# The dispatch logits of the first eight token tiles are made at the head of attention instead of at the start of dispatch

## The chip, the cores and the metric

The kernel runs on one core of a Trainium2 chip. The metric is the device time of one execution in microseconds (us), the median of the runs. The core has a tensor engine (TensorE, PE in the rows), a vector engine (VectorE, DVE), a scalar engine (ScalarE, ACT), GpSimd (POOL) and SyncE (SP), whose queue issues nearly all DMA transfers here. Each engine works through its own instructions in order and waits on semaphores.

## What is computed

A transformer block in fp32 on x of shape (4, 2048, 256): causal grouped-query attention (16 heads of 16, four groups of keys and values), and beside it a soft mixture of 16 experts with 64 slots each. Both read the layer norm of x.

```python
att = jnp.einsum('bsgmd,btgd->bgmst', q, k) / scale      # causal, softmax, times v, times wo
logits = jnp.einsum('bnd,esd->bnes', x, se)              # 2048 tokens x 1024 slots per batch
dispatch = jax.nn.softmax(logits, axis=1)                # over tokens
combine = jax.nn.softmax(logits.reshape(b, n, -1), axis=-1)   # over slots
slots = jnp.einsum('bnd,bnes->besd', x, dispatch)
gate = gelu(slots @ Wg + bg); up = slots @ Wu + bu; eout = (gate * up) @ Wd + bd
out = x + attention + combine @ eout
```

## The kernel before

There are five blocks, and all engines meet between them: `project` (norm, queries, keys, values; it also stores the normed and turned tokens as `y_cols`), `attend`, `dispatch`, `experts`, `combine`.

`attend` handles 16 pairs of batch and key group (`bg`), each in 40 steps, so steps 0 to 639, with a lead of 22 steps (-22 to -1) ahead. `program(s)` lists what TensorE does in step s: four products of keys and queries (`"s"`, L890), whose exponentials ScalarE takes (L809), four products of queries and keys whose row maxima VectorE takes (`"x"`, L903, L857 and L863), and the products with the values of two steps before (`"a"`, L932). The maxima run 22 steps ahead of the products that use them, so the lead holds only maxima: 88 of them. Results go through a ring of seven PSUM banks (`att_ring`), filled in the order of the program; whoever fills a bank waits for the reader of what was in it. When the last maximum of a chunk of 512 queries is made, GpSimd splits the negated maxima in two parts (L778, L780), TensorE turns them three steps later (`"m"`, L909), VectorE copies them (L874), and SyncE writes them as extra rows into the queries (L719). In the lead that happens for chunk 0 in step -16 and for chunk 1 in step -8.

The queries and keys of key groups 1 to 3 have rows that must be zero. ScalarE sets them with twelve copies at the head of `attend` (L799, L801). SyncE loads group 1 in step -6, group 2 in step 6, group 3 in step 46 (`FIRST_LOADS`, `load_group`, L528 to L537): 17 transfers each.

`dispatch` makes, per batch, the logits of 16 tiles of 128 tokens x 1024 slots (phase `"L"`): per tile twelve products on TensorE (L1246: two halves of the slots, two halves of D, three of high and low parts), one copy on ScalarE (L1108), one exponential on ScalarE (L1081, stored as `slot_exps`), and on VectorE one row maximum (L1166) and one running column maximum (L1174). It then multiplies with the tokens (phase `"P"`). The order is L0, L1, P0, L2, P1 and so on. The columns come in chunks of four tiles in three buffers (`yTl`, `yTh`), which GpSimd splits into a high and a low part; the first three chunks are loaded and split at the end of `attend` (L733, L746, L748).

Of the kernel before, what the change touches and what calls it, by code (L numbers as in the profile page):

```python
# [46 lines left out]
HL = GS // NRG  # L47
VW = 32
# [43 lines left out]
def project(nc, w, io, scr, g0):  # L92
# [3 lines left out]
    with ExitStack() as ctx:  # L96
        a = Alloc(nc, ctx, "proj")
        passed = a.sem("passed")
        x = a.sb("x", [P, NX, TPC, D])
        xn = a.sb("xn", [P, 2, TPC, D])  # L100
# [5 lines left out]
        part = a.sb("part", [P, 2, 3, 2, CH], F32R)  # L106
# [413 lines left out]
def load_group(sp, scr, b, g, qs, ks, v, loaded, zeroed):  # L520


    for j in range(len(Q_PART)):
        for rg in range(NRG):
            r = slice(RG * rg + HD * j, RG * rg + HD * (j + 1))
            if b == 0 and zeroed and HD * j >= 32:
                sp.wait_ge(zeroed, 2 * NRG)
# [12 lines left out]
def attend(nc, w, scr, g0, cols):  # L540
# [37 lines left out]
    FIRST_LOADS = {-6: 1, 6: 2, 46: 3}  # L578
    first = [u for u in range(NU) if u == 0 or UNITS[u - 1][0] != UNITS[u][0]]
# [71 lines left out]
    with ExitStack() as ctx:  # L651
        a = Alloc(nc, ctx, "att")
        passed = a.sem("passed")
        qs = [g0["qs"]] + [a.sb(f"qs{g}", [P, CPB, HL * CH], F32R) for g in range(1, NKV)]
# [16 lines left out]
        zeroed = [sem(f"zeroed{g}") for g in range(NKV)]  # L671
# [4 lines left out]
        acc_zeroed, v_ones = sem("acc_zeroed"), sem("v_ones")  # L676
        (sT_ready, exp_done, mask_done, pv_done, mb_ready, mb_used, m_step, nm_ready,
# [4 lines left out]
        def wait_bank(pe, e):  # L682
# [3 lines left out]
            kept = [x[1] * CPB + x[2] + 1 for x in before.get(e, ()) if x[0] == "c"]  # L686
            if exps:
                pe.wait_ge(exp_done, max(exps))
# [9 lines left out]
        with nc.Block() as block:  # L698
            @block.sync
            def _(sp):  # L700
                def load(b, g):
                    for _ in load_group(sp, scr, b, g, qs[g], ks[g], v[g], loaded[g], zeroed[g]):
                        pass
# [5 lines left out]

                for s in ALL_STEPS:  # L710
                    if s in FIRST_LOADS:
                        load_first(FIRST_LOADS[s])
                    for e in program(s):
# [7 lines left out]
                        elif e[0] == "c":  # L721
# [4 lines left out]
                                         cn[:, c]).then_inc(c_out[c], 16)  # L726
                    bg = (s - AV_LAG) // NU
# [3 lines left out]
                    if s == STEPS - NU:  # L731
                        for n in range(RING):
                            sp.dma_start(cols["low"][:, n].bitcast(F32),  # L733
                                         scr["yT_in"][n // CPB, n % CPB]).then_inc(cols["in"][n], 16)
# [4 lines left out]
            def _(pool):  # L739
                def split_columns(k):  # L740

                    n, d = divmod(k, DK)
                    hi, lo = cols["high"][:, n, d], cols["low"][:, n, d]
                    if d == 0:
                        pool.wait_ge(cols["in"][n], 16)
# [4 lines left out]

                for g in range(NKV):
                    nc.gpsimd.memset(v[g][:, :, HD, :], 1.0).then_inc(v_ones, 1)
                for s in ALL_STEPS:
                    if STEPS - 8 * RING * DK // 2 <= s < STEPS and (s - STEPS) % 4 == 0:
# [29 lines left out]
            def _(act):  # L784
# [10 lines left out]
                for g in range(1, NKV):  # L795
                    for rg in range(NRG):
                        r = slice(RG * rg + 32, RG * (rg + 1))
                        zero = w["causal"][r, 0:1]
                        nc.scalar.copy(qs[g][r].rearrange("p c n -> p (c n)"),  # L799
                                       zero.to_broadcast([32, CPB * HL * CH])).then_inc(zeroed[g], 1)  # L800
                        nc.scalar.copy(ks[g][r], zero.to_broadcast([32, S])).then_inc(zeroed[g], 1)  # L801
                for s in ALL_STEPS:
                    if 0 <= s < STEPS:
# [19 lines left out]
            def _(dve):  # L823
# [18 lines left out]
                nc.vector.memset(acc[:], 0.0).then_inc(acc_zeroed, 1)  # L842
                for s in ALL_STEPS:
# [859 lines left out]
```

## Time and profile before

| | us |
|---|---|
| median of three runs | 2695.19 (2692.81 to 2697.54) |
| the profiled execution, its own time | 2698.62 |
| its span in the profile | 2696.9 |
| `project` | 0 to 157 |
| `attend`: lead, then steps 0 to 639 | 159 to 202, 202 to 1760 |
| `dispatch`: L0, L1, then the rest | 1762 to 1809, 1809 to 1873, to about 2215 |
| granted TensorE clock, mean | 0.98 |

The table is in microseconds from the first instruction. A granted clock of 1.0 is 2.4 GHz, 0.5 is 1.2 GHz. Times of instructions are those of one profiled execution.

### The profile page before, as it was taken

The numbers are of one execution on the slowest core, as the hardware profiler recorded it, in microseconds if no ns is written. First come the engines' busy times: TensorE is split into PE (matmuls) and PEld (weight loads), VectorE is DVE, ScalarE is ACT, GpSimd is POOL, SyncE is SP. The second block draws the span as 40 slices with busy tenths as digits, with TensorE's granted clock in tenths as the row PEclk, the third lists the DMA queues.
The fourth block names the chain that finished last, engine by engine and source line by source line (L and its number), as shares of the span: only waits on it lengthen the run. The fifth ranks groups of instructions, "written<-read, shape, count | busy, mean of one in ns | idle before, by whom it ended". The sixth has DMA issues, their size and how long they took to land. (4 is left out here: it accounts for less than half of the span.)

```text
span 2696.9 us, 47797 instructions
## 1 busy us (share of the span) xinstructions
PE 2583.9 (96%) x16291; PEld 1542.2 (57%) x16291; DVE 2048.5 (76%) x4879; ACT 1728.3 (64%) x3510; POOL 427.1 (16%) x676
## 2 busy tenths in 40 slices
PE   7989999999999999999999999998989989999999
PEld 4544444444444444444444444376877878889999
DVE  7779889989998998998898998477465513356665
ACT  4567777777777777777777777966666652222221
POOL 6701111111111111111111111323120100100000
PEclk9969999999999999999999999999999999999999
DMA  7945423303312321330330000044333354545654
GB/s 247 324 111 60 58 29 45 44 12 41 45 24 27 45 34 17 45 44 6 45 44 6 10 6 31 7 181 168 124 134 145 102 168 147 175 152 194 194 193 151
DMA packets 175855, 245.10 MB, mean 91 GB/s; under 512 B 57205, under 2 KB 129017, under 8 KB 174105
## 3 DMA queue, kind: packets, MB, share of 16 engines
q1 hardware_dynamic: 160088, 227.73, 33.8%
q10 hardware_dynamic: 15552, 14.68, 1.8%
q8 instruction: 114, 1.87, 0.3%
q14 instruction: 101, 0.82, 0.1%
HBM read 156.21 MB, written 84.97 MB: 89 GB/s over the span
## 5 line engine op out<-in xcount | busy, mean ns | idle before, releaser
L809 ACT ACTIVATE att_pr<-att_ring 128x512 f32<-128x512 f32 (+3 forms) x2560 | 1174.3, 550 | 333.9 <-PE att_ring L890 326.6
L857 DVE TENSOR_REDUCE att_mx<-att_ring 128x1 f32<-128x512 f32 x1536 | 967.5, 679 | 76.6 <-PE att_ring L903 74.2
L903 PE MATMUL att_ring<-att_ks,att_qs 48*128 48x512 f32 (+3 forms) x1920 | 648.4, 422 | 16.3 <-ACT att_pr L809 7.0
L890 PE MATMUL att_ring<-att_qs,att_ks 64*128 64x512 f32 (+3 forms) x1920 | 578.2, 407 | 5.8 <-DVE att_mx L863 2.3
L890 PEld LDWEIGHTS att_ring<-att_qs,att_ks 64*128 64x128 f32 x1920 | 300.5, 186 | 402.7 <-DVE att_mx L857 148.3
L863 DVE CUSTOM_DVE_ANT_0 att_junk<-att_ring,w_causal 128x256 bf16<-128x256 f32 (+3 forms) x1024 | 466.1, 486 | 59.5 <-PE att_ring L903 34.1
L932 PE MATMUL att_acc<-att_pr,att_v 128*17 128x512 f32 (+3 forms) x3840 | 454.3, 544 | 3.9 <-ACT att_cT L820 1.5
L903 PEld LDWEIGHTS att_ring<-att_ks,att_qs 48*128 48x128 f32 x1920 | 306.9, 185 | 141.6 <-ACT att_pr L809 102.0
L760 POOL TENSOR_SCALAR_AFFINE_SELECT att_pr<-att_pr 128x512 f32<-128x512 f32 x256 | 162.5, 635 | 1035.5 <-ACT att_pr L809 1035.4
L903 PE MATMUL att_ring<-g_ks,g_qs 48*128 48x512 f32 (+3 forms) x640 | 227.1, 465 | 15.6 <-PEq L152 5.7
L1513 ACT CAST com_e1h<-com_tp 128x1024 fp32r<-128x1024 f32 x64 | 64.8, 1017 | 236.2 <-PE com_tp L1573 236.2
L890 PE MATMUL att_ring<-g_qs,g_ks 64*128 64x512 f32 (+3 forms) x640 | 198.4, 410 | 2.5 <-DVE att_mx L863 0.8
L1589 PE MATMUL com_mp<-pre_parts,com_e1h 128*128 x1024 | 186.3, 282 | 4.0 <-DVE com_e1l L1538 4.0
L890 PEld LDWEIGHTS att_ring<-g_qs,g_ks 64*128 64x128 f32 x640 | 103.6, 188 | 135.1 <-DVE att_mx L857 51.3
L1589 PEld LDWEIGHTS com_mp<-pre_parts,com_e1h 128*128 128x128 f32 x1024 | 158.4, 190 | 4.8 <-issue 4.8
L932 PE MATMUL att_acc<-att_pr,g_v 128*17 128x512 f32 (+3 forms) x1280 | 152.0, 547 | 0.0
L903 PEld LDWEIGHTS att_ring<-g_ks,g_qs 48*128 48x128 f32 x640 | 110.7, 201 | 68.5 <-ACT att_pr L809 29.3
L1589 PE MATMUL com_mp<-pre_parts,com_e1l 128*128 x512 | 144.5, 282 | 0.0
L932 PEld LDWEIGHTS att_acc<-att_pr,att_v 128*17 128x17 f32 x3840 | 78.2, 117 | 114.4 <-ACT att_pr L809 72.8
L1246 PE MATMUL dis_ps<-w_seTh,w_yTh 128*128 128x512 f32 x256 | 106.1, 414 | 20.1 <-ACT dis_lg L1108 11.1
L1263 PE MATMUL dis_ps<-dis_y,dis_lg 128*128 128x257 f32 x512 | 114.9, 386 | 7.3 <-ACT dis_lg L1061 7.3
L1263 PE MATMUL dis_ps<-dis_y,pre_parts 128*128 128x257 f32 x512 | 112.6, 380 | 4.5 <-ACT pre_parts L1061 4.5
(170 smaller groups left out, 3272.5 us busy)
## 6 DMA issues: line engine op xcount, KB each, us to landing
slot_exps<-dis_e SPq DMA_DIRECT2D x64, 512.0 KB, 2.7
com_e<-slot_exps SPq DMA_DIRECT2D x64, 512.0 KB, 3.5
att_qs<-q_parts SPq DMA_DIRECT2D x72, 256.0 KB, 12.0
q_parts<-proj_part SPq DMA_DIRECT2D x32, 512.0 KB, 5.1
dis_y<-in_L_attn_x_dram SPq DMA_DIRECT2D x64, 256.0 KB, 2.8
att_ks<-k_parts SPq DMA_DIRECT2D x72, 128.0 KB, 12.6
y_cols<-proj_yT SPq DMA_DIRECT2D x16, 512.0 KB, 5.5
context<-att_cn SPq DMA_DIRECT2D x64, 128.0 KB, 2.0
```

Source lines behind the costliest of these rows:

```text
L760: nc.gpsimd.affine_select(out=blk, in_=blk, compare_op=ALU.is_ge, fill=0.0, base=0, pattern=[[0, GS], [1, P]], channel_multiplier=-1).then ...
L809: nc.scalar.activation(pr[:, s % NPR, h, off:CH], spot(("s", s, h)), ACT.Exp, scale=float(HD) ** -0.5).then_inc(exp_done, 1)
L857: nc.vector.tensor_reduce(dst, spot(e), AX.X, ALU.max).then_inc(mb_used, 1)
L863: nc.vector.tensor_tensor_reduce(junk[:, h % 2, 0:wd], spot(e), w["causal"][:, CH - wd:CH], 1.0, LOW, ALU.add, ALU.max, dst).then_inc(mb_u ...
L890: nc.tensor.matmul(spot(e), ks[g][r, kb * P:(kb + 1) * P], qs[g][r, c, hf * CH + off:(hf + 1) * CH], start=True, stop=True).then_inc(sT_re ...
L903: nc.tensor.matmul(spot(e), qs[g][r, c, q0:q0 + P], ks[g][r, j * CH:j * CH + wd], start=True, stop=True).then_inc(mb_ready, 1)
L932: last = nc.tensor.matmul(acc[VW * h:VW * h + HD + 1, off:CH], v[bg % NKV][:, kb // TPC, :, kb % TPC], pr[:, n % NPR, h, off:CH], start=(n ...
L1246: last = nc.tensor.matmul(ps[:, i % 2, 2 * (t % 2) + h, :], lhs[:, n % RING, k, (t % TPC) * P:(t % TPC + 1) * P], w[rhs][:, k, h * 512:(h ...
L1263: last = nc.tensor.matmul(ps[:, i % 2, q, 0:D + 1], lgs[b % 2][:, t, (hf * HB + q) * P:(hf * HB + q + 1) * P], y[:, m % NY, t % 2, 0:D + 1 ...
L1513: nc.scalar.copy(e1h[:, q].rearrange("p s n -> p (s n)"), tp[:, q, 0:2, :].rearrange("p a n -> p (a n)")).then_inc(e1h_kept, 1)
L1589: last = nc.tensor.matmul(mp[:, q, 0:D], lhs[:, q, s, :], rhs[:, b, s, :], start=(s == 0 and rhs is eoh and lhs is e1h), stop=(s == SB - 1 ...
```

## The change

Eight tiles (`NE`), two chunks of columns, of batch 0 leave phase L0.

- At the head of `attend`, SyncE loads their two chunks of columns, GpSimd splits them, and steps -18 to -3 each get one entry `"l"`: six products that make half a tile of logits (512 slots) in one bank of the ring. ScalarE copies each to the buffer of the exponentials, which is idle in the lead, and SyncE stores each in a new DRAM tensor `first_logits`. ScalarE waits at step 0 until all 16 stores have landed.
- At the end of `attend`, SyncE loads these logits into the queries of key groups 0 and 1, which are done with, and VectorE takes the row and column maxima of the eight tiles in the steps that have no maxima of attention left.
- In `dispatch`, SyncE loads the eight tiles again, to where phase P reads them. L0 makes tiles 8 to 15 only. The exponentials of all 32 tiles of L0 and L1 are spread over the 24 tiles that are left.
- The twelve copies that set rows to zero become twelve GpSimd memsets: two ahead of the column split, the others one per step from step -22 on, ahead of the split of the maxima of that step.
- The queries of the four groups are one tensor, `queries`; a buffer of `project` lies in it, and `nr` and `cm` move to where both blocks reach them.

```diff
+NE = 8
+NEC = NE // TPC
@@ attend
+    NL = 2 * NE
+    L_FROM = -LEAD + 4
@@ program(s)
+        early = [("l", s - L_FROM)] if 0 <= s - L_FROM < NL else []
-        out = [st[0], xs[0], st[1], xs[1]] + ev + [xs[2], st[2], st[3], xs[3]] + av
+        out = [st[0], xs[0], st[1], xs[1]] + ev + [xs[2], st[2], st[3], xs[3]] + early + av
@@ SyncE
+                for n in range(NEC):
+                    sp.dma_start(cols["low"][:, n].bitcast(F32), scr["yT_in"][0, n]).then_inc(cols["in"][n], 16)
                 for s in ALL_STEPS:
                     if s in FIRST_LOADS:
                         load_first(FIRST_LOADS[s])
...
+                        elif e[0] == "l":
+                            k = e[1]
+                            sp.wait_ge(l_kept, k + 1)
+                            sp.dma_start(scr["first_logits"][k // 2, :, k % 2 * 512:(k % 2 + 1) * 512],
+                                         half_tile(k)).then_inc(l_out, 16)
...
+                    if s == STEPS - NU + AV_LAG:
+                        sp.wait_ge(l_out, 16 * NL)
+                        sp.wait_ge(pv_done, (NBG - 4 + -(-NE // 4)) * NU)
+                        for t in range(NE):
+                            sp.dma_start(lg[:, t, :], scr["first_logits"][t]).then_inc(l_in, 16)
@@ GpSimd
+                side = zeros()
+                for _ in range(2):
+                    next(side)
+                for n in range(NEC):
+                    pool.wait_ge(cols["in"][n], 16)
+                    hi, lo = cols["high"][:, n], cols["low"][:, n]
+                    nc.gpsimd.tensor_copy(hi, lo.bitcast(F32)).then_inc(l_split, 1)
+                    pool.wait_ge(l_split, 2 * n + 1)
+                    nc.gpsimd.tensor_tensor(lo, lo.bitcast(F32), hi.bitcast(F32), ALU.subtract).then_inc(l_split, 1)
+                    pool.wait_ge(l_split, 2 * n + 2)
...
                 for s in ALL_STEPS:
+                    if s < 0:
+                        made = sum(len(m_events(u)) for u in range(-LEAD, s))
+                        if made:
+                            pool.wait_ge(nm_ready, made)
+                        next(side, None)
@@ ScalarE
+                    for e in program(s):
+                        if e[0] == "l":
+                            act.wait_ge(mb_ready, turn[e] + 1)
+                            if e[1] >= NPR * GS:
+                                act.wait_ge(l_out, 16 * NPR * GS)
+                            nc.scalar.copy(half_tile(e[1]), spot(e)).then_inc(l_kept, 1)
+                    if s == 0:
+                        act.wait_ge(l_out, 16 * NL)
@@ VectorE: logit_maxes() waits for l_in, then a row maximum and a column maximum per tile, 16 instructions;
@@ one of them per step without maxima, two in odd steps
@@ dispatch
+        first_tile = lambda b: 0 if b else NE
+        SLOTS = 2 * TPB - NE
+        exps_by = lambda b, t: min(-(-2 * TPB * (b * TPB + t + 1 - NE) // SLOTS), b * TPB + t)
+                for t in range(NE):
+                    sp.dma_start(lgs[0][:, t, :], scr["first_logits"][t]).then_inc(l_in[min(t, 1)], 16)
...
+                    if b == 0 and t < 2:
+                        act.wait_ge(l_in[t], 16 if t == 0 else 16 * (NE - 1))
```

How the program's order changes, at three places. First GpSimd from the start of `attend` to the first split of maxima. Before:

```order
L738 UNCONDITIONAL_BRANCH
L752 MEMSET g_v 128x4x4
L752 MEMSET att_v 128x4x4 x3
L778 CAST att_nml<-att_nm 128x2x8
L780 TENSOR_TENSOR att_nml<-att_nm,att_nml 128x2x8
```

And now, in the changed program (`w_queries` and `att_ks` are the zeroed rows):

```order
L791 MEMSET w_queries 32x4096
L789 MEMSET att_ks 32x2048 [waits att_zeroed]
L801 CAST w_yTh<-w_yTl 128x1024 [waits w_yT_in0,att_zeroed]
L803 TENSOR_TENSOR w_yTl<-w_yTl,w_yTh 128x1024 [waits att_l_split]
L801 CAST w_yTh<-w_yTl 128x1024 [waits w_yT_in1,att_l_split]
L803 TENSOR_TENSOR w_yTl<-w_yTl,w_yTh 128x1024 [waits att_l_split]
L806 MEMSET g_v 128x4x4 [waits att_l_split]
L806 MEMSET att_v 128x4x4 [waits att_v_ones] x3
L791 MEMSET w_queries 32x4096 [waits att_v_ones]
L789 MEMSET att_ks 32x2048 [waits att_zeroed]
L791 MEMSET w_queries 32x4096 [waits att_zeroed]
L789 MEMSET att_ks 32x2048 [waits att_zeroed]
L838 CAST att_nml<-att_nm 128x2x8 [waits att_nm_max,att_zeroed]
```

The first split of maxima, which came behind four small memsets, now stands behind six large memsets and two column splits.

Second, TensorE in steps -17 and -16 of the changed program (L982 are products for maxima, L991 to L993 the logits, L999 the turn of chunk 0's maxima; before, the L982 kind and L999's stand alone):

```order
L982 MATMUL att_ring<-g_ks,w_queries 128x512 [waits att_mb_used] x4
L991 MATMUL att_ring<-w_seTh,w_yTh 128x512 [waits att_l_split,att_mb_used]
L992 MATMUL att_ring<-w_seTl,w_yTh 128x512
L993 MATMUL att_ring<-w_seTh,w_yTl 128x512
L991 MATMUL att_ring<-w_seTh,w_yTh 128x512
L992 MATMUL att_ring<-w_seTl,w_yTh 128x512
L993 MATMUL att_ring<-w_seTh,w_yTl 128x512
L982 MATMUL att_ring<-g_ks,w_queries 128x512 [waits att_mb_used]
L982 MATMUL att_ring<-g_ks,w_queries 128x512 [waits att_l_kept]
L999 MATMUL att_ring<-w_ident,att_nml 32x128 [waits att_nm_ready,att_mb_used]
L982 MATMUL att_ring<-g_ks,w_queries 128x384 [waits att_mb_used] x2
```

All that follows in TensorE's order stands behind the wait for the split columns and the wait for the split maxima.

Third, SyncE around step -6 of the changed program (L750 are the stores of logits, L532 to L541 the load of group 1, of which six alternating pairs stand there):

```order
L739 DMA w_queries<-att_mrow 2x8x128 [waits att_mb_used]
L739 DMA w_queries<-att_mrow 2x8x128
L750 DMA first_logits<-att_pr 128x512 [waits att_l_kept] x2
L532 DMA w_queries<-q_parts 16x4x1024
L533 DMA att_ks<-k_parts 16x2048
...
L534 DMA att_v<-v_rows 128x4x64
L541 DMA att_ks<-w_ones 1x32x64 x4
L750 DMA first_logits<-att_pr 128x512 [waits att_l_kept] x4
```

Twelve stores are issued ahead of the load of group 1, the last four behind its 17 transfers.

## Rows read from the trace of the kernel before

**Rows 1.** The page: busy time, share of the span, instructions.

```profile
PE 2583.9 (96%) x16291; PEld 1542.2 (57%) x16291; DVE 2048.5 (76%) x4879; ACT 1728.3 (64%) x3510; POOL 427.1 (16%) x676
```

**Rows 2.** Windows: stretch, length, busy by engine, then clock, DMA share, GB/s.

```profile
200.00:205.00 5.00, 4.98 (x10) 2.28 (x9) 5.00 (x13) 1.19 (x2) 0.00 (x0) 0.50 0.98 109
210.00:220.00 10.00, 9.79 (x65) 4.01 (x63) 9.04 (x23) 7.04 (x17) 2.04 (x5) 0.81 0.41 44
```

**Rows 3.** Timeline of TensorE in the lead: start, us, engine, line, operation.

```profile
158.95 3.50 PE L903 MATMUL att_ring<-g_ks,g_qs 48*128 48x256 f32 x13 [5.73 <-PEq L152]
162.93 3.06 PE L903 MATMUL att_ring<-g_ks,g_qs 48*128 48x384 f32 x8 [0.48 <-DVE att_mx L863]
...
169.01 0.40 PE L909 MATMUL att_ring<-w_ident,att_nml 128*32 128x128 f32 x1
...
202.22 0.76 PE L890 MATMUL att_ring<-g_qs,g_ks 64*128 64x512 f32 x1
```

**Rows 4.** Timeline of VectorE: chunk 1's first maximum, chunk 2's first, first idle time.

```profile
166.53 0.69 DVE L857 TENSOR_REDUCE att_mx<-att_ring 128x1 f32<-128x512 f32 x1
...
183.95 0.68 DVE L857 TENSOR_REDUCE att_mx<-att_ring 128x1 f32<-128x512 f32 x1
...
212.99 0.42 DVE L863 CUSTOM_DVE_ANT_0 att_junk<-att_ring,w_causal 128x256 bf16<-128x256 f32 x1 [0.96 <-PE att_ring L903]
```

**Rows 5.** Timeline of ScalarE at step 0: its first exponentials.

```profile
203.01 0.60 ACT L809 ACTIVATE att_pr<-att_ring 128x512 f32<-128x512 f32 x1 [11.58 <-PE att_ring L890]
...
205.82 1.25 ACT L809 ACTIVATE att_pr<-att_ring 128x512 f32<-128x512 f32 x3 [1.07 <-PE att_ring L890]
```

**Rows 6.** Timeline of GpSimd: its memsets in `project`, a column split in `dispatch`.

```profile
24.41 3.50 POOL L329 MEMSET g_qs<- 32x4096 f32 x1
34.84 1.84 POOL L332 MEMSET g_ks<- 32x2048 f32 x1
...
1790.62 1.04 POOL L1193 CAST w_yTh<-w_yTl 128x1024 fp32r<-128x1024 f32 x1 [6.40 <-DMA w_yTl<-y_cols]
1791.74 2.41 POOL L1195 TENSOR_TENSOR w_yTl<-w_yTl,w_yTh 128x1024 fp32r<-128x1024 f32 x1
```

**Rows 7.** Timeline of SyncE's queue: group 2's first transfer, a store behind it.

```profile
217.79 0.40 SPq L528 DMA_DIRECT2D att_qs<-q_parts  x1
...
227.88 0.58 SPq L725 DMA_DIRECT2D context<-att_cn  x1
```

**Rows 8.** DMA issues with KB and us to landing: 188 to 240 us, whole span.

```profile
context<-att_cn SPq DMA_DIRECT2D x1, 128.0 KB, 13.7
...
context<-att_cn SPq DMA_DIRECT2D x64, 128.0 KB, 2.0
```

**Rows 9.** Timelines of TensorE and ScalarE in L0.

```profile
1762.19 0.76 PE L1246 MATMUL dis_ps<-w_seTh,w_yTh 128*128 128x512 f32 x1 [3.95 <-PEq L698]
...
1767.35 1.01 ACT L1108 COPY pre_parts<-dis_ps 128x1024 f32<-128x1024 f32 x1 [8.69 <-PE dis_ps L1246]
...
1773.86 1.15 ACT L1081 ACTIVATE dis_e<-pre_parts,dis_nr 128x1024 f32<-128x1024 f32 x1
...
1809.35 1.02 ACT L1108 COPY pre_parts<-dis_ps 128x1024 f32<-128x1024 f32 x1 [0.65 <-PE dis_ps L1246]
```

**Rows 10.** Windows: the fastest stretch of loads, in `project`.

```profile
9.00:12.00 3.00, 2.05 (x10) 1.65 (x9) 2.63 (x11) 1.64 (x6) 2.29 (x8) 1.00 1.07 333
```

**Rows 11.** End of attention: timelines of SyncE and VectorE.

```profile
1655.93 1.35 SPq L733 DMA_DIRECT2D w_yTl<-y_cols  x3
...
1719.36 0.28 DVE L874 CAST att_mrow<-att_ring 32x128 fp32r<-32x128 f32 x1 [3.58 <-PE att_ring L909]
1733.71 0.25 DVE L840 RECIPROCAL att_rz<-att_cc 128x16 f32<-128x16 f32 x1 [14.07 <-ACT att_cc L792]
```

**Rows 12.** L1: ScalarE's eight norms in one go, TensorE's wait behind them.

```profile
1833.81 4.04 ACT L1071 ACTIVATE dis_y<-dis_y,w_yb,w_ys 128x256 f32<-128x256 f32 x8
...
1838.80 0.50 PE L1246 MATMUL dis_ps<-w_seTh,w_yTh 128*128 128x512 f32 x1 [1.48 <-ACT dis_lg L1108]
```

More of the change, by code:

```diff
@@ L47 @@
 HL = GS // NRG
+NE = 8
+NEC = NE // TPC
+QW = CPB * HL * CH
 VW = 32
@@ L670, in attend @@
         loaded = [g0["loaded"]] + [sem(f"loaded{g}") for g in range(1, NKV)]
-        zeroed = [sem(f"zeroed{g}") for g in range(NKV)]
+        zeroed = sem("zeroed")
         m_rows = [sem(f"m_rows{c}") for c in range(CPB)]
@@ L686, in wait_bank @@
             kept = [x[1] * CPB + x[2] + 1 for x in before.get(e, ()) if x[0] == "c"]
+            early = [x[1] + 1 for x in before.get(e, ()) if x[0] == "l"]
+            if early:
+                pe.wait_ge(l_kept, max(early))
             if exps:
@@ L904, in _ @@
                                              ks[g][r, j * CH:j * CH + wd], start=True, stop=True).then_inc(mb_ready, 1)
+                        elif e[0] == "l":
+                            t, h = divmod(e[1], 2)
+                            wait_bank(pe, e)
+                            pe.wait_ge(l_split, 2 * (t // TPC) + 2)
+                            at, to = slice(t % TPC * P, (t % TPC + 1) * P), slice(h * 512, (h + 1) * 512)
+                            for k in range(DK):
+                                hi, lo = cols["high"][:, t // TPC, k, at], cols["low"][:, t // TPC, k, at]
+                                nc.tensor.matmul(spot(e), hi, seTh[:, k, to], start=(k == 0), stop=False)
+                                nc.tensor.matmul(spot(e), hi, seTl[:, k, to], start=False, stop=False)
+                                last = nc.tensor.matmul(spot(e), lo, seTh[:, k, to], start=False, stop=(k == DK - 1))
+                            last.then_inc(mb_ready, 1)
                         elif e[0] == "m":
@@ L936, in _, with dispatch @@
                             last.then_inc(pv_done, 1)
-def dispatch(nc, w, io, scr, pre, cols):
+def dispatch(nc, w, io, scr, pre, cols, first_logits):
     HB = SB // 2
@@ L957, in dispatch @@
         e1 = a.sb("e1", [P, 2, NS])
-        nr, zr = a.sb("nr", [P, 2, TPB]), a.sb("zr", [P, 2, TPB])
-        cm = a.sb("cm", [P, 2, NS])
+        nr, cm, nr_ready, cm_done = (first_logits[n] for n in ("nr", "cm", "nr_ready", "cm_done"))
+        zr = a.sb("zr", [P, 2, TPB])
         rz = a.sb("rz", [P, SB])
@@ L1026, in _ @@
                         b = ph[1]
-                        for t in range(TPB):
+                        for t in range(first_tile(b), TPB):
                             if t % TPC == TPC - 2:
@@ L1073, in norm_rows, with token_exps @@
                         normed = m + 1
+                exps = 0
+                def token_exps(stop):
+                    nonlocal exps
+                    for n in range(exps, stop):
+                        token_exp(n // TPB, n % TPB)
+                    exps = max(exps, stop)
                 def token_exp(b, t):
+                    if b == 0 and t < 2:
+                        act.wait_ge(l_in[t], 16 if t == 0 else 16 * (NE - 1))
                     act.wait_ge(nr_ready, b * TPB + t + 1)
@@ L1160, in _ @@
                             slots(i - 1, turned)
-                        for t in range(TPB):
-                            n = b * TPB + t
+                        for t in range(first_tile(b), TPB):
+                            n = b * TPB + t - NE
                             dve.wait_ge(lg_ready, n + 1)
@@ L1206, in _ @@
                         column_maxes(b - 1)
-                    for n in range(b * CPB, b * CPB + CPB):
+                    for n in range(b * CPB if b else NEC, b * CPB + CPB):
                         split(n + RING)
@@ L1607, in block_kernel @@
     s_d = dram("slots", [B - 1, SB, P, D])
+    l_d = dram("first_logits", [NE, P, NS])
     io = {
@@ L1670, in block_kernel @@
                    "parts": parts}
-            dispatch(nc, w, io, scr, pre, cols)
+            dispatch(nc, w, io, scr, pre, cols, first_logits)
             com = combine_inputs(late, nc, io, scr)
```

129 lines of the change are left out of this document (86 added, 43 removed).

## The prediction

> **What bounds the kernel now.** I read the page first: TensorE is busy for 96% of the span [rows 1], so work taken from it should pay, but a share is an average over stages. So I read windows and timelines of the two places the change touches. In the lead the reader is to see that TensorE runs at 1.2 GHz and that VectorE has no gap (5.00 of 5.00 us busy [rows 2]): the maxima set the pace. Chunk 1's eight steps take VectorE from 166.53 to 183.95, 2.18 us a step [rows 4]. VectorE stays gapless until its first idle 0.96 us at 212.99 [rows 4], so everything that holds it up between 159 and 213 lengthens the kernel. After that, TensorE and VectorE are both nearly full [rows 2], and no slack further on takes up a delay. In L0 TensorE is the bound: ScalarE waits for it 0.65 us per tile, and the copies run from 1767.35 to 1809.35 for 15 tiles, 2.80 us a tile [rows 9], so a half tile costs 1.40 us at 2.4 GHz. At 1.2 GHz I take six times 512 columns, 2.6 us.
>
> **Head, part 1: the split columns.** GpSimd starts at 158.9 and does 3.50 + 1.84 (memsets) + 1.04 + 2.41 (split of chunk 0) [rows 6]; with about 0.1 between, the first logits may start at 168.0. The columns themselves land by then (512 KB, issued at once). TensorE gets there after 20 products, at about 165.7 [rows 3]. It waits 2.3 us, and the half tile takes until 170.6. Step -17 follows: four products (1.7) and a half tile (2.6 or less), then two products of step -16: about 175.
>
> **Head, part 2: the split maxima.** In step -16 TensorE must turn chunk 0's maxima. GpSimd goes on from 168.0 with chunk 1's split (3.6), four small memsets (0.8) and the four memsets of steps -22 to -19 (3.50 + 1.84 + 3.50 + 1.84, with gaps 11.0) [rows 6], and only then splits the maxima (0.5): 183.9. Before, TensorE turned them at 169.01 [rows 3]. It now waits some 9 us, with everything behind it, and turns them at 184.0: 15.0 late. VectorE runs dry meanwhile.
>
> **Head, part 3: the rest of the lead.** Before, 33.2 us passed from there to step 0 (169.01 to 202.22 [rows 3]). After: TensorE comes from an idle stretch, so at 1.2 GHz: the rest of step -16 and step -15 are 3.3 + 3.8, less about 1 if the clock rises within it: 6. Then twelve steps with four products and a half tile at 2.4 GHz: 0.8 + 1.4 = 2.2, about VectorE's own 2.18, so 26.6; the two steps without logits 4.4. Sum 37.0: step 0 starts at 221.0 against 202.2, 18.8 late. The second turn (step -8, about 203) is not late: GpSimd's last six memsets end at about 201. ScalarE's zeroing is no gain, since it waited for 11.58 us ahead of the first exponential anyway [rows 5].
>
> **Head, part 4: the stores behind group 1's load.** ScalarE may not start step 0 before all 16 stores have landed. SyncE issues the load of group 1 at step -6, when logits 11 are kept: 221.0 less 4.4 less 9.0 (steps -6 to -3), plus the copy, so 208.4. The last four stores are issued behind it. What such a store costs shows at group 2's load: its first transfer is issued at 217.79, and the context store behind its 17 transfers, at 227.88 [rows 7], lands 13.7 us later, where the median of such stores is 2.0 [rows 8]. That is 23.8 us after the load began. The four stores bring 1 MB more, 3 us at 333 GB/s [rows 10]. So ScalarE starts at 208.4 + 23.8 + 3 = 235.2, where its input would have been there at 221.8: 13.4 us of wait. Queued behind it are all exponentials, behind these the ring, so TensorE after seven banks, and VectorE. Two things come back. When ScalarE starts, step 0's products stand ready, and four exponentials take 2.1 us instead of the 4 from 203.01 on [rows 5], and TensorE had filled three maxima more: 2.5 together. And before, TensorE stayed at 1.2 GHz for another ten us [rows 2], of which VectorE felt 0.96 (idle at 212.99 [rows 4]); I count 1.5. The head is then later by (235.2 + 0.7) - (203.0 + 0.7) - 2.5 - 1.5 = **28 us**.
>
> The Trainium skill ("DMA: Bandwidth & Descriptors", section "Queues, rings and completion order") says that each DMA engine consumes the descriptors of a queue in ring order, but that completion is not first in, first out for an issuing engine. By its first half the stores wait as here and the trace agrees (13.7 us against 2.0); by its second half a store could land ahead of the load's last transfers, which is the first rival.
>
> **End of attention: 0.** SyncE is far ahead there: it issues the columns at 1655.93, and the 4 MB of logits would follow at once, 14 us at 300 GB/s. VectorE needs them at 1716. Its 16 instructions of about 1.2 us lie in its idle time (14.07 us ahead of 1733.71 and more behind [rows 11]). The last copy of maxima (1719.36 [rows 11]) has four of them ahead, 4.0 us from 1715.7: at most 0.5 us late, and its rows are needed only at step 624, some 5 us later. If that cover were gone it would cost up to 3 us.
>
> **Dispatch.** L0 loses eight tiles of 2.80 us: -22.4. But ScalarE's second exponential waits for the reload of 4.2 MB. At 333 GB/s, the fastest stretch of the trace [rows 10], that is 12.6 us, with 2.7 for start and landing 15.3 us after 1762.2. Timeline from there: tile 8 at 1.2 GHz until 5.2 (as now, 1767.35 [rows 9]), tile 9 until 7.9, tile 10 until 10.6; tile 11 needs tile 9's copy, which ScalarE makes behind the second exponential (1.15 [rows 9]): 15.3 + 1.2 + 1.0 = 17.5. TensorE has idled for 7 us, so tile 11 costs about 5.0, then four tiles 11.2: L0 ends at 33.7 against 47.1 now (1809.35 [rows 9]): **-13.4**. Afterwards 4 exponentials fall to 3 tiles: 0.91 + 1.33 x 1.15 = 2.45 us of ScalarE per tile, under 2.80, so hidden; the eight norms in one go (4.04 us), behind which TensorE waits 1.48 us now [rows 12], meet one exponential more, +1.2, and pairs of exponentials may wait for stores of `slot_exps`, +0.2. Dispatch: **-12**.
>
> **Sum.** +28 - 12 = +16 us. The profiled execution took 2698.6 (span 2696.9 and 1.7 around it), 3.4 above the median; against itself that gives 2714.6, against the median of 2695.2 the forecast is **2711 us**, 0.6% slower.
>
> **Bounds.** Reload: landed as fast as TensorE needs it (within 9 us) dispatch gives -22.3 + 1.4 = -21; at half the rate (28 us) it gives 0. Store wait: 0 to 17 us. GpSimd's chain has prices of the same forms, so 1 to 2 us either way.
>
> **Rivals.**
> (1) *Not slower: the stores pass the load.* If the last stores land before 221.8, part 4 is gone. Then VectorE is later only by parts 1 to 3, 18.8, less what the ended 1.2 GHz stretch gave up and TensorE's lead over VectorE at step 0 (4 us): 14.5, and the sum is +2.5: 2698, within what can be told. It decides if they land within 5 us of issue (issued at 208.4 plus 8 to 10 us of SyncE's own issuing). For it: only four stores, on all DMA engines. Against: [rows 8]. With a reload that lands early it even ends faster, 2689.
> (2) *TensorE stays at 1.2 GHz through the whole lead.* Each of 14 steps costs 4.1 instead of 2.2 us: +27 on the head, some of it hidden under the store wait's own start: 2735. For it: the clock was 0.5 for the whole lead, TensorE not full [rows 2]. Against: with logits TensorE is the bound and never idle, and in L0 it rose inside 5 us from such a start [rows 9].
> (3) *The reload at dispatch is slower than the fastest stretch*, at 200 GB/s: the first exponentials wait 8 us more, 2719.
>
> **Chances.** Forecast with its range 2703 to 2720: 0.66. Rival 1: 0.14, of which half faster. Rival 2: 0.06. Rival 3: 0.10. Left, the change pays after all by gains I don't see: 0.04. A measurement of this kernel tells 0.2% (5 us) from no change. So faster 0.09, same 0.07, slower 0.84; the range 2698 to 2726 leaves out rival 2 and the faster cases.
>
> **What would show it.** After: a wait of TensorE of 2 to 3 us on the column split near 166, and of about 9 us on GpSimd's split of maxima, turned near 184; step 0 of TensorE near 221; ScalarE's first exponential near 235 behind a DMA; stores of `first_logits` with landings above 20 us for the last ones; in L0 a ScalarE wait of about 8 us on DMA and TensorE idle for 7; L0's end 33 to 35 us after dispatch begins. I am wrong if the last stores land within some us, if the clock is 0.5 up to step 0, or if VectorE finds slack between 220 and 1700.

## The result, and the profile after

The changed kernel takes 2723.74 us (median of four runs, 2722.26 to 2725.43) against 2696.36 for the kernel before (four runs): a ratio of 1.0099, 95% interval 1.0087 to 1.0112, so 1.0% slower. A second series, beside four of the experiments, gave 1.0114 (1.0097 to 1.0131; e5_after_again below).

Where the 24 us of the profiled execution (span 2721.0 against 2696.9) went shows in landmarks. Since `project`, whose work is the same in all kernels, ends anywhere from 154.6 to 161.8 us in the executions told of here, I count from the start of attention (TensorE's first product of maxima), and dispatch from its first product to that of the experts.

| us | before | after |
|---|---|---|
| TensorE's step 0 after attention's start | 43.3 | 59.2 |
| ScalarE's first exponential after it | 44.1 | 76.4 |
| attention, to its last turn (`att_cT`, four products on TensorE) | 1598.7 | 1628.7 |
| dispatch, to its last copy of L0 | 47.2 | 35.4 |
| dispatch, to its last copy of L1 | 106.5 | 99.4 |
| dispatch, whole | 454.5 | 448.6 |

The timeline of TensorE in the lead, which answers to [rows 3] (start, us, engine, line, operation, and in brackets the idle time before it and what ended it):

```profile
157.08 3.50 PE L982 MATMUL att_ring<-g_ks,w_queries 48*128 48x256 f32 x13 [5.69 <-PEq L156]
166.07 0.77 PE L991 MATMUL att_ring<-w_seTh,w_yTh 128*128 128x512 f32 x1 [2.77 <-DVE att_mx L936]
181.70 0.37 PE L999 MATMUL att_ring<-w_ident,att_nml 128*32 128x128 f32 x1 [8.89 <-POOL att_nml L840]
216.29 0.47 PE L969 MATMUL att_ring<-w_queries,g_ks 64*128 64x512 f32 x1 [0.26 <-DVE att_mx L942]
234.16 0.96 PE L982 MATMUL att_ring<-g_ks,w_queries 48*128 48x512 f32 x2 [13.83 <-ACT att_pr L870]
```

Three waits stand in it that were not there before: 2.77, 8.89 and 13.83 us. The first is put down to VectorE, but VectorE had been done; the products wait for the split columns as well, and GpSimd ends that split at 165.9. Its timeline, answering to [rows 6]:

```profile
157.04 3.50 POOL L791 MEMSET w_queries<- 32x4096 f32 x1 [22.83 <-POOLq L156]
160.60 1.80 POOL L789 MEMSET att_ks<- 32x2048 f32 x1
162.46 1.04 POOL L801 CAST w_yTh<-w_yTl 128x1024 fp32r<-128x1024 f32 x1
163.58 2.34 POOL L803 TENSOR_TENSOR w_yTl<-w_yTl,w_yTh 128x1024 fp32r<-128x1024 f32 x1
...
175.63 3.50 POOL L791 MEMSET w_queries<- 32x4096 f32 x1
179.19 1.80 POOL L789 MEMSET att_ks<- 32x2048 f32 x1
181.06 0.20 POOL L838 CAST att_nml<-att_nm 128x16 fp32r<-128x16 f32 x1
181.33 0.22 POOL L840 TENSOR_TENSOR att_nml<-att_nm,att_nml 128x16 fp32r<-128x16 f32 x1
```

GpSimd never waits between 157 and 181: it is late with the maxima's split only by what stands ahead of it. The third wait starts at the stores. SyncE's queue and ScalarE, answering to [rows 5] and [rows 7]:

```profile
206.46 1.27 SPq L532 DMA_DIRECT2D w_queries<-q_parts  x1
...
213.37 2.46 SPq L541 DMA_DIRECT2D att_ks<-w_ones  x4
215.87 3.54 SPq L750 DMA_DIRECT2D first_logits<-att_pr  x4
```

```profile
214.26 0.59 ACT L861 COPY att_pr<-att_ring 128x512 f32<-128x512 f32 x1 [1.66 <-PE att_ring L993]
233.51 2.23 ACT L870 ACTIVATE att_pr<-att_ring 128x512 f32<-128x512 f32 x5 [18.66 <-DMA first_logits<-att_pr]
```

The last half tile is kept at 214.85, its store is issued by 219.4, and the first exponential starts at 233.51. What the transfers do meanwhile shows in windows of two us (length, busy by engine, clock, DMA share, GB/s):

```profile
226.00:228.00 2.00, 0.00 (x0) 0.00 (x0) 0.00 (x0) 0.00 (x0) 0.00 (x0) 0.50 1.02 109
228.00:230.00 2.00, 0.00 (x0) 0.00 (x0) 0.00 (x0) 0.00 (x0) 0.00 (x0) 0.50 1.27 112
230.00:232.00 2.00, 0.00 (x0) 0.00 (x0) 0.00 (x0) 0.00 (x0) 0.00 (x0) 0.50 1.05 364
```

No compute engine is busy. The DMA engines are full at 110 GB/s with the load's small packets until 230 (1028 of the 2437 packets from 202 to 240 are under 512 bytes), and only then do the four stores run, at 364 GB/s.

In dispatch the timelines answer to [rows 9] and [rows 12]. ScalarE, then TensorE:

```profile
1796.09 1.02 ACT L1228 COPY pre_parts<-dis_ps 128x1024 f32<-128x1024 f32 x1 [8.92 <-PE dis_ps L1366]
...
1803.37 1.15 ACT L1201 ACTIVATE dis_e<-pre_parts,w_nr 128x1024 f32<-128x1024 f32 x1 [5.13 <-DMA pre_parts<-first_logits]
...
1807.81 1.15 ACT L1201 ACTIVATE dis_e<-pre_parts,w_nr 128x1024 f32<-128x1024 f32 x1 [2.30 <-DMA slot_exps<-dis_e]
...
1815.69 1.15 ACT L1201 ACTIVATE dis_e<-pre_parts,w_nr 128x1024 f32<-128x1024 f32 x1 [2.54 <-DMA slot_exps<-dis_e]
...
1824.87 1.15 ACT L1201 ACTIVATE dis_e<-pre_parts,w_nr 128x1024 f32<-128x1024 f32 x1 [1.74 <-DMA slot_exps<-dis_e]
```

```profile
1805.56 0.50 PE L1366 MATMUL dis_ps<-w_seTh,w_yTh 128*128 128x512 f32 x1 [3.76 <-ACT pre_parts L1228]
1817.88 0.50 PE L1366 MATMUL dis_ps<-w_seTh,w_yTh 128*128 128x512 f32 x1 [2.02 <-ACT pre_parts L1228]
1831.44 0.50 PE L1366 MATMUL dis_ps<-w_seTh,w_yTh 128*128 128x512 f32 x1 [2.10 <-ACT dis_lg L1228]
1860.78 0.80 PE L1366 MATMUL dis_ps<-w_seTh,w_yTh 128*128 128x512 f32 x1 [5.78 <-ACT dis_lg L1228]
```

One wait of ScalarE is for the reload; nine more in L0 and L1 are for stores of `slot_exps`, 0.64 to 2.75 us each, and TensorE waits behind them for copies. Before, L0 had no such wait and L1 one of 0.35 us.

Only dispatch as a whole is a sharp landmark. In the seven executions that leave it as changed, L0's end lies 35.3 to 37.8 us into dispatch and L1's end 99.4 to 101.8, so the two middle rows of the table can't be read closer than 2.5 us.

### The profile page after: what moved, and what is told of

It is laid out like the page before. It is cut to its first block and busy times, and to the rows that moved or that the text cites. A ratio compares the mean times of both kernels' runs of the same rounds, so it can differ in the third digit from the quotient of the medians.

```text
span 2721.0 us, 47868 instructions
## 1 busy us (share of the span) xinstructions
PE 2573.9 (95%) x16291; PEld 1533.1 (56%) x16291; DVE 2038.8 (75%) x4879; ACT 1696.3 (62%) x3506; POOL 464.2 (17%) x688
## 5 line engine op out<-in xcount | busy, mean ns | idle before, releaser
L982 PE MATMUL att_ring<-att_ks,w_queries 48*128 48x512 f32 (+3 forms) x1920 | 647.5, 422 | 16.9 <-ACT att_pr L870 7.6
L969 PE MATMUL att_ring<-w_queries,att_ks 64*128 64x512 f32 (+3 forms) x1920 | 575.9, 406 | 7.2 <-DVE att_mx L942 2.3
L969 PEld LDWEIGHTS att_ring<-w_queries,att_ks 64*128 64x128 f32 x1920 | 300.8, 186 | 403.3 <-DVE att_mx L936 144.5
L982 PEld LDWEIGHTS att_ring<-att_ks,w_queries 48*128 48x128 f32 x1920 | 307.2, 185 | 142.7 <-ACT att_pr L870 104.1
L982 PE MATMUL att_ring<-g_ks,w_queries 48*128 48x512 f32 (+3 forms) x640 | 207.0, 434 | 25.4 <-ACT att_pr L870 15.7
L969 PE MATMUL att_ring<-w_queries,g_ks 64*128 64x512 f32 (+3 forms) x640 | 197.3, 409 | 3.3 <-DVE att_mx L942 1.1
L969 PEld LDWEIGHTS att_ring<-w_queries,g_ks 64*128 64x128 f32 x640 | 103.5, 187 | 136.6 <-DVE att_mx L936 51.0
L982 PEld LDWEIGHTS att_ring<-g_ks,w_queries 48*128 48x128 f32 x640 | 98.6, 191 | 71.6 <-ACT att_pr L870 43.0
L1366 PE MATMUL dis_ps<-w_seTh,w_yTh 128*128 128x512 f32 x224 | 94.6, 422 | 33.4 <-ACT dis_lg L1228 16.6
```

The source lines that it names most:

```text
L969: nc.tensor.matmul(spot(e), ks[g][r, kb * P:(kb + 1) * P], qs[g][r, c, hf * CH + off:(hf + 1) * CH], start=True, stop=True).then_inc(sT_re ...
L982: nc.tensor.matmul(spot(e), qs[g][r, c, q0:q0 + P], ks[g][r, j * CH:j * CH + wd], start=True, stop=True).then_inc(mb_ready, 1)
L1366: last = nc.tensor.matmul(ps[:, i % 2, 2 * (t % 2) + h, :], lhs[:, n % RING, k, (t % TPC) * P:(t % TPC + 1) * P], w[rhs][:, k, h * 512:(h ...
```

## The experiments

Twelve runs were made: eleven altered kernels, and the changed kernel once more. Each ran beside the kernel before. A ratio is good to about 0.2% (5 us). The first exponential's place is sharper: in the five executions with an unaltered head it lies at 76.4 to 77.7 us. So is dispatch: of the seven executions that leave it as changed, six lie at 448.1 to 448.7 and one (e9_other_queue) at 445.9. Attention as a whole varies by up to 9 us among equal heads (1624.9 to 1633.7).

| label | ratio to before | first exponential | attention | dispatch |
|---|---|---|---|---|
| before | 1 | 44.1 | 1598.7 | 454.5 |
| after | 1.0099 | 76.4 | 1628.7 | 448.6 |
| e1_zeros_late | 1.0098 | 68.5 | 1622.1 | 448.7 |
| e2_load_late | 1.0066 | 61.2 | 1617.6 | 448.6 |
| e3_both | 1.0032 | 53.0 | 1611.2 | 448.5 |
| e4_four_buffers | 1.0083 | 77.7 | 1633.7 | 437.4 |
| e5_after_again | 1.0114 | 76.7 | 1624.9 | 448.2 |
| e6_stores_first | 1.0076 | 77.5 | 1632.1 | 443.8 |
| e7_tile_waits | 1.0100 | 77.3 | 1628.1 | 448.0 |
| e8_all | 0.9954 | 46.3 | 1601.2 | 438.1 |
| e9_other_queue | 1.0105 | 74.4 | 1624.0 | 445.9 |
| e10_before_four_buffers | 1.0006 | 44.1 | 1598.2 | 454.9 |
| e11_all_stores_first | 0.9969 | 47.8 | 1604.9 | 437.6 |
| e12_zeros_step16 | 1.0066 | 63.1 | 1613.8 | 448.1 |

The last three columns are in microseconds, counted as in the table above, from the one profiled execution of each run. The interval of each ratio is 0.0010 to 0.0024 to either side.

### The head: GpSimd's order and the load

e1_zeros_late:

```diff
                 side = zeros()
-                for _ in range(2):
-                    next(side)
...
-                        next(side, None)
+                        if s >= -18:
+                            next(side, None)
```

> The changed kernel, with only GpSimd's order in attention's head altered: the first two memsets no longer stand ahead of the columns' split, and the twelve of them stand at steps -18 to -7 instead of -22 to -13, behind the first split of the maxima; group 1's four are still done long before its load. Theory (GpSimd's queue is what makes TensorE late at the first logits and at the first turn of maxima): the 2.77 us idle ahead of the first logits product and the 8.89 us ahead of the first turn shrink to under 1 us each, the stretch at half clock behind them goes with them, and the landmark at the end of attention comes 10 to 12 us earlier; about 2712. Rival A (the time is set by the stores of the half tiles alone, so a lead that is quicker only waits longer at the first exponential): the wait of 13.8 us ahead of the maxima at step 0 grows by what the lead gives back, and the time stays at 2723. Rival B (a memset now stands in the way of the second split): a wait of about 3 us at the second turn, so about 2715.

Measured: TensorE's waits in the lead of this kernel.

```profile
165.11 0.76 PE L990 MATMUL att_ring<-w_seTh,w_yTh 128*128 128x512 f32 x1 [0.69 <-POOL w_yTl L801]
192.18 0.37 PE L998 MATMUL att_ring<-w_ident,att_nml 128*32 128x128 f32 x1 [3.65 <-POOL att_nml L839]
227.36 0.96 PE L981 MATMUL att_ring<-g_ks,w_queries 48*128 48x512 f32 x2 [12.92 <-ACT att_pr L869]
```

The two waits go (0.69 us is left of the first). The first exponential comes 7.9 us sooner and the end of attention 6.6, not 10 to 12, because eight memsets now stand ahead of the second turn and cost a new wait of 3.65 us (Rival B's). The ratio alone can't tell it from the changed kernel's.

e2_load_late, and e3_both with both edits:

```diff
-    FIRST_LOADS = {-6: 1, 6: 2, 46: 3}
+    FIRST_LOADS = {-2: 1, 6: 2, 46: 3}
```

> The changed kernel, with only the load of group 1 moved in SyncE's queue from step -6 to step -2, behind the last four stores of half tiles. Theory (the first exponential waits for the last four stores, and these stand behind the load's issues, its wait for GpSimd's memsets and its transfers): ScalarE's first exponential comes about 14 us earlier, the idle of 13.8 us at TensorE ahead of the products of maxima goes, and the time is 2709 to 2712. Rival (the stores' own completion, or the rows of maxima behind the load, hold the same place): the first exponential comes at most 3 us earlier and the time is 2720 to 2724.

> Both edits of the two kernels above. Theory (two waits one after the other on the path): they add, 23 to 26 us less than the changed kernel, 2698 to 2701. If the two hide one another the time is 2708 to 2712. What is then left against the kernel before is the logits' own work in the lead (16 half tiles of some 1.4 us on TensorE) less what dispatch gives back.

Measured, ScalarE's first exponential in e2_load_late:

```profile
220.51 1.09 ACT L870 ACTIVATE att_pr<-att_ring 128x512 f32<-128x512 f32 x2 [2.84 <-DMA first_logits<-att_pr]
```

It comes 15.3 us sooner (61.2 against 76.4; the theory said 14) and attention is 11 us shorter, by one execution each. Some of the difference is what a late start gives back (see part 4 below), which is now lost again. In e3_both the two add, 23.4 us at the first exponential and 17.5 us of attention. The ratio of 1.0032 is 18 us below the 1.0099 (22 us below the second series' 1.0114), against 23 to 26 expected.

e12_zeros_step16 is e1_zeros_late with `s >= -16`, so that six memsets and not eight stand ahead of the second turn.

> The changed kernel, with only the memsets moved as in the version with all edits: from step -16 on, six of them ahead of the second split of the maxima, where the first experiment had eight and a wait of 3.65 us with half clock behind it. Group 1's load stays at step -6. Theory (GpSimd's queue costs 14 to 15 us of the lead, the last four stores behind the load another 13 to 15, and the two add): no wait over 1 us at the logits or at either turn, step 0 at 45 to 46 us after attention's start instead of 59.2, the first exponential 16 to 17 us behind it, at 61 to 63 instead of 76.4, a ratio of 1.005 to 1.007. Rival (a quicker lead only meets the load's transfers, so the stores land when they land): the first exponential at 66 or later, a ratio of 1.007 or more.

Measured: no wait of TensorE over 0.74 us up to step 0, step 0 at 46.6, the first exponential at 63.1, 13.3 us sooner than in the changed kernel; ratio 1.0066 (1.0049 to 1.0082). So GpSimd's queue costs 13 us there by itself, and the load 15 by itself. Both together cost 30, as e8_all shows.

### What the last stores wait for

e9_other_queue:

```diff
 # SyncE
+                            if k >= NL - 4:
+                                continue
 # ScalarE, behind the copy
+                            if k >= NL - 4:
+                                act.wait_ge(l_kept, k + 1)
+                                act.dma_start(scr["first_logits"][k // 2, :, k % 2 * 512:(k % 2 + 1) * 512],
+                                              half_tile(k)).then_inc(l_out, 16)
```

> The changed kernel, with only the stores of the last four half tiles issued by ScalarE, each behind its copy, and not by SyncE behind group 1's load. In the changed kernel they are issued 215.9 to 219.4 us and the last has landed at 233.5, 14 us later. Theory Q (what they wait for is their place behind the load, at SyncE and in the rings): issued at some 208 to 215, they land within 3 us of the last, so that the first exponential starts at about 217 to 219 instead of 233.5 and the time is 10 to 13 us shorter than the changed kernel's, some 2710. Theory D (what they wait for is the DMA engines, which the load's transfers fill from 206 on at a share of 0.9 and more, whoever issues): a store from another queue shares the engines with the load and lands late too; the first exponential comes at 226 or later and the time is at most 6 us shorter.

Measured, timeline of ScalarE and its queue, then windows:

```profile
213.33 0.33 ACTq L867 DMA_DIRECT2D first_logits<-att_pr  x1
229.02 2.23 ACT L877 ACTIVATE att_pr<-att_ring 128x512 f32<-128x512 f32 x5 [15.72 <-DMA first_logits<-att_pr]
```

```profile
220.00:222.00 2.00, 0.00 (x0) 0.00 (x0) 0.00 (x0) 0.00 (x0) 0.00 (x0) 0.50 1.11 207
224.00:226.00 2.00, 0.00 (x0) 0.00 (x0) 0.00 (x0) 0.00 (x0) 0.00 (x0) 0.50 1.04 183
226.00:228.00 2.00, 0.00 (x0) 0.00 (x0) 0.00 (x0) 0.00 (x0) 0.00 (x0) 0.50 1.02 203
```

Theory D. The last store is issued by 213.7 and not behind the load, yet it lands some 15 us later. Of the four, the first, issued when the load had just begun, landed in 7.8 us, the other three in 14.9 to 16.8. The stretches from 220 to 228 now carry 163 to 207 GB/s, where the changed kernel had about 110 and then 364, so stores and load do run mixed; but the engines' share is 1.0 either way, and both are done at about the same time after the load's first transfer: 24.1 us (from 204.91) against 27.05 (from 206.46). The place in the queue is worth 2 us, the load's hold on the DMA engines the rest. The Trainium skill ("DMA: Bandwidth & Descriptors", section "Queues, rings and completion order") says that a DMA engine takes turns between the queues that have work, one packet at a time. That the rates mix agrees with it.

### Dispatch: buffers, order, waits

e4_four_buffers gives the exponentials of L0 and L1 two more buffers, in the space of `sl` and `slT`, which are first written in P0:

```diff
+        spare = [sl.rearrange("p q d -> p (q d)"), slT.rearrange("p q e k j -> p (q e k j)")]
+        def e1_at(n):
+            if n >= 2 * TPB:
+                return n % 2, 16 * (TPB // 2 + (n - 2 * TPB) // 2), e1[:, n % 2]
+            return n % 4, 16 * (n // 4) + (32 if n % 4 >= 2 else 0), (e1[:, n % 4] if n % 4 < 2 else spare[n % 4 - 2])
...
-                    if b * TPB + t >= 2:
-                        act.wait_ge(e_out[t % 2], 16 * ((b * TPB + t) // 2))
+                    q, landed, to = e1_at(b * TPB + t)
+                    if b * TPB + t >= 4:
+                        act.wait_ge(e_out[q], landed)
```

> The changed kernel, with only the buffers of the token exponentials altered in the first two L phases of dispatch: four instead of two (the two spare ones lie in the space of the slots, which is not used before the first P phase). Theory (dispatch gave back 5.8 us of the 12 forecast because ScalarE's exponentials wait for the stores of slot_exps, 0.6 to 2.7 us at a time): these waits go, L0 is about 4 us and L1 about 3 to 4 us shorter, and the time is 2715 to 2718. Rival (ScalarE is not what bounds L0 and L1; TensorE with its waits for the banks or the splits is): the waits go, and the time stays within 2 us of 2723.

Measured: TensorE waits once in L0, for the reload, and not again until the eight norms in L1.

```profile
1809.12 0.80 PE L1378 MATMUL dis_ps<-w_seTh,w_yTh 128*128 128x512 f32 x1 [5.34 <-ACT pre_parts L1238]
```

The end of L1 comes 92.4 us into dispatch, where the changed kernel had 99.4, and dispatch is 11.2 us shorter, more than the 7 to 8 expected. (The whole time can't tell: the ratio gives 4 us with an interval that holds 0 and 9, and the profiled execution is 8 us shorter with an attention that happened to be 5 us longer.) Its control, the same edit in the kernel before:

> A control: the kernel before the change, with four buffers for the exponentials in L0 and L1 as in the experiment on the changed kernel. Theory (the wait on the stores of slot_exps is the changed kernel's own, made by four exponentials to every three tiles in L0 and L1): dispatch stays within 1 us of its 454.5 us and the ratio is 0.999 to 1.001. Rival (the kernel before is held by its two buffers as well): dispatch is 3 us or more shorter and the ratio under 0.999; what the last version gains over the kernel before is then partly not the change's.

Measured: dispatch 454.9 against 454.5, ratio 1.0006 (0.9996 to 1.0016). But for 0.35 us once, the kernel before does not wait for these stores; the wait belongs to the change.

e6_stores_first: in SyncE's loop over tiles of L0 and L1, `store_exps(exps_by(b, t))` stands ahead of `load_yT(...)`.

> The changed kernel, with only SyncE's order in L0 and L1 of dispatch altered: the stores of the token exponentials that a step owes stand ahead of that step's load of columns, which waits for TensorE's products of a later tile. With four buffers dispatch became 11.2 us shorter. Theory S (the stores are late because SyncE is held by the columns' wait): most of that comes back here too, dispatch 7 to 11 us shorter, 2710 to 2714 on this chip. Theory B (two buffers are too few for a store that takes 2 to 4 us to land, wherever it stands): dispatch at most 4 us shorter, 2716 to 2720.

Measured: dispatch 4.8 us shorter, between the two theories. The first wait on a store is 3.14 us even so, later ones 0.6 to 2.1. So the order alone takes away some 5 of the 11 us that two more buffers take away. It adds nothing to the buffers (e11_all_stores_first below), so the two don't split the 11 us between them. Since one unaltered dispatch was 2.7 us short of the rest, the 5 is rough.

e7_tile_waits lets the exponentials of tiles 1 to 3 wait for a semaphore each instead of one for all seven (in short):

```diff
-                        act.wait_ge(l_in[t], 16 if t == 0 else 16 * (NE - 1))
+                        act.wait_ge(*l_on[t])
```

> The changed kernel, with only the waits for the reloaded logits in dispatch altered: the exponential of each of tiles 1 to 3 waits for its own tile, not for all seven that follow the first. Theory (ScalarE's second exponential, held until the whole reload has landed, holds the copy behind it and so TensorE's third tile for 3.76 us): that idle time goes and dispatch is 2 to 4 us shorter, 2716 to 2718. Rival (the exponentials then run into the stores of slot_exps earlier, as there are two buffers): the 3.76 us go and come back as waits on the stores, within 1 us of no change.

Measured, ScalarE's third exponential:

```profile
1809.54 1.15 ACT L1202 ACTIVATE dis_e<-pre_parts,w_nr 128x1024 f32<-128x1024 f32 x1 [8.84 <-DMA slot_exps<-dis_e]
```

The rival: the wait for the reload goes, and the third exponential waits 8.84 us for the store of the first, which was issued behind the reload's 4.2 MB and four loads of tokens. Dispatch 448.0 against 448.6.

### Everything together

e8_all has e12_zeros_step16's memsets, the late load, the tile waits and the four buffers; e11_all_stores_first has SyncE's stores first in place of the tile waits. e5_after_again is the changed kernel.

> The changed kernel once more, as it was, to have its time against the kernel before on the chip of the experiments. Expected: the ratio of 1.0099 again, about 2720 on a chip where the kernel before takes 2693.

> All edits together: memsets from step -16 on, six ahead of the second split of the maxima instead of eight; group 1's load at step -2; a wait for each of the reloaded tiles 1 to 3; four buffers for the exponentials in L0 and L1. Sum by the traces: 17.5 us (both edits of the head together, in attention), 11.2 us (buffers, in dispatch), about 3 us (tile waits), and 3 to 4 us of the idle and half clock at the second turn of the maxima: 35 us below the changed kernel, 2684 to 2688 on a chip where the kernel before takes 2693, a ratio of 0.996 to 0.998. If the gains in dispatch hide one another (the exponentials are bound by one thing at a time) it is 2688 to 2693, no change against the kernel before.

> The version with all edits, without the separate waits for the reloaded tiles (they moved a wait and took none away), and with the stores of the exponentials ahead of the load of columns in SyncE's queue. Dispatch was 437.4 us with four buffers alone and 438.1 with the tile waits beside them. Theory (with four buffers the order still costs a little: a load of columns holds SyncE for up to one tile): 0 to 3 us shorter than the version with all edits, ratio to the kernel before 0.994 to 0.996. Rival (four buffers cover the order; the columns now come later and GpSimd's split with them): no change or up to 2 us longer, ratio 0.995 to 0.997.

Measured for e8_all: 2683.6 us, ratio 0.9954 (0.9939 to 0.9969), which is 0.5% faster than the kernel before and a little better than the 0.996 to 0.998 expected. TensorE and ScalarE in its lead, and a window:

```profile
166.92 0.77 PE L990 MATMUL att_ring<-w_seTh,w_yTh 128*128 128x512 f32 x1 [0.74 <-POOL w_yTl L801]
205.54 0.46 PE L968 MATMUL att_ring<-w_queries,g_ks 64*128 64x512 f32 x1 [0.26 <-DVE att_mx L941]
```

```profile
206.23 0.60 ACT L869 ACTIVATE att_pr<-att_ring 128x512 f32<-128x512 f32 x1 [2.12 <-DMA first_logits<-att_pr]
```

```profile
195.00:200.00 5.00, 5.00 (x26) 3.08 (x23) 4.84 (x13) 1.49 (x3) 4.88 (x3) 1.00 0.29 108
```

Attention started at 159.96, so the first exponential is at 46.3: sixteen half tiles of logits cost the lead 2.2 us (3.7 in e11_all_stores_first, whose head is the same). TensorE, at full clock instead of the 0.50 of [rows 2], fits them beside the maxima, and VectorE stays nearly full (4.84 of 5.00). Dispatch is 438.1, so the tile waits add nothing to the buffers. e11_all_stores_first: 2688.1 us, ratio 0.9969 (0.9959 to 0.9980), dispatch 437.6. That is in the rival's range: there is no gain from the order once there are four buffers.

## Why the prediction was right, and where not

The forecast was 2711, the median 2724: outside the 2703 to 2720 that had a chance of 0.66, inside the wider 2698 to 2726. The sign holds, and so does the mechanism of the head; the sum was +16 and the two traces give +24. (Three small slips of the sum change nothing: twelve steps of 2.2 are 26.4 and not 26.6, four are 8.8 and not 9.0, and the chances listed add up to 0.11 for faster, not 0.09.)

**Head, part 1 (wait 2.3 us) and part 2 (turn 15.0 late).** Right: 2.77 us, and 8.89 us at the turn, which is 24.6 us after attention's start where the text had 25.0. That GpSimd's queue is the cause is shown by e1_zeros_late and e12_zeros_step16.

**Part 3 (37.0 us from the turn to step 0).** It took 34.6. The two steps without logits were mis-sized: TensorE makes their eight products in one go from 214.16 and is at step 0 2.1 us later, not 4.4. The slip does not reach the first exponential, because the load and the stores decide that, and the load's first transfer is issued 49.4 us after attention's start, as in the text (49.5).

**Part 4 (stores behind the load).** Right in its size: 27.05 us from the load's first transfer to the first exponential, 23.8 + 3 in the text; the first exponential is 76.4 after the start, 76.3 in the text. What came back was 4.0 in the text. Here the first chunk's copy (`att_cT`) comes 2.9 us sooner after the first exponential than before, the fifth 4.1. In the four other executions with this head it is 2.5 for the first and 2.1 to 3.7 for the fifth, so 4.0 was some 1 us too much. The reason given for the wait was half right. The stores stand behind the load in the queue, as the bytes of 230 to 232 show, but e9_other_queue shows that another queue saves 2 us only; the load fills the DMA engines for over 20 us. e2_load_late shows that it is the load: with the load behind the stores, the first exponential comes 15.3 us sooner.

**Rival 1** (stores pass the load) did not happen: they ran after it. **Rival 2** (1.2 GHz through the lead) did not either: the clock was 1.00 from 190 to 215, after stretches of 0.50 with the waits. **Rival 3** (a slower reload) failed in the other direction: the second exponential started 12.8 us into dispatch, the text had 15.3, and TensorE idled 3.76 us and not 7.

**Head, sum (+28).** Attention's last turn came 28.2 us later than before in the time of the span. That it meets the 28 so closely is luck: in its own length attention grew by 30.0, and by 26.2 to 35.0 in the five executions with this head, and `project` happened to be 1.9 shorter. The end of attention cost 1.2 us at most: the last copy of maxima was 27.0 us late, the last turn 28.2.

**Dispatch (-12) is the term that was mis-sized.** It gave 5.8. L0's end was 11.7 us nearer to dispatch's start, not 13.4, with a reload that was faster than assumed; L1 lost 4.7 of it again (4.7 to 7.0 in the seven executions with this dispatch) where the text had 1.2 + 0.2. The step that failed: "pairs of exponentials may wait for stores of `slot_exps`, +0.2". I had looked at ScalarE's busy time per tile (2.45 of 2.80 us) and not at its two buffers: spread as four exponentials to three tiles, they come in pairs, each needs the store of two before, and SyncE issues that store behind a load that waits for TensorE. With four buffers dispatch gives 17.1 (e4_four_buffers), and e10_before_four_buffers shows that none of this was there before. So +0.2 should have been 7 to 9 by the end of L1 and 11 in all. The other terms of dispatch were too small by 5, since without this wait it gives 17.1 and not 12: 14.1 by the end of L1, and 3.0 in the phases behind it, for which the text had nothing. What makes these 3.0 no run shows.

The two traces differ by 24.1, 8 more than the sum: 6 of that is dispatch, and 1.5 lies behind it (the experts start 22.6 late), in code that is the same. It is no scatter: from the experts' first product to the end it is 480.3 us in the kernel before and in e10_before_four_buffers, and 481.4 to 482.5 in all twelve executions of the changed kernel and its variants. Its cause is open. The medians differ by 27.4; the other 3.3 is that the profiled execution of before was 2.3 us above its median and that of after 1.0 below.

## What to carry to other kernels

Moving work into a gap is priced by the queues that feed it. Here the moved products cost 2 to 4 us by themselves; the memsets ahead of a 0.4 us split and one bulk load beside the stores cost 30. List what stands ahead of each short instruction that somebody waits for, on every engine. When producers are packed more densely, check the number of buffers and the issuing order of their stores, not their busy time.

## What was not expected of the hardware

A store of 256 KB with large rows, issued on a queue of its own while another queue's load of small packets held the DMA engines (share 1.0, 110 GB/s), took 15.3 us to land (median of four), against 2.4 us for two such stores just ahead of the load (e9_other_queue, DMA issues from 200 to 240 us):

```profile
first_logits<-att_pr ACTq DMA_DIRECT2D x4, 256.0 KB, 15.3
first_logits<-att_pr SPq DMA_DIRECT2D x2, 256.0 KB, 2.4
```

In the mixed stretches the engines moved 163 to 207 GB/s. Issued behind the load on the same queue, the stores moved at 364 GB/s, but only when the load was done.
